# Moved weight splits and a reordered opening of attention in a gated cross-attention block

## The reference, cut to what matters

```python
x = x + tanh(g_xattn[0]) * xattn(layernorm(x), ctx, ctx, Wq, bq, Wk, bk, Wv, bv, interference, amp, Wo, bo)
x = x + tanh(g_ffn[0]) * ffn(layernorm(x), W_org, lora_down, lora_up, lora_keys, Wq)
...
def xattn(q, k, v, ...):
    qh, kh, vh = (interfere(proj(t, W, b)) for t, W, b in ...)   # x @ W.T + b, then a 4x4 mix per head
    weights = softmax(einsum('bhqdm,bhkdm->bhqkm', qh, kh) / sqrt(dk), axis=3)
    out = einsum('bhqkm,bhkdm->bhqdm', weights, vh)
    return out.reshape(b, s, dm) @ Wo.T + bo
```

## Time and profile before

| | us |
|---|---|
| median of the runs | 1349.94 (1349.28 to 1350.39) |
| profiled execution, its own time | 1349.01 |
| span of the profiled execution | 1347.2 |
| PE busy in the span | 1327.0 |
| DVE / POOL / ACT busy | 704.2 / 566.8 / 409.4 |

### The profile page before, as it was taken

How to read it: one execution, slowest core, us unless ns; L and a number is a source line. 1 busy time by engine, 2 the same in 40 slices (tenths; PEclk the granted TensorE clock), 3 DMA queues, 4 the chain that set the end, 5 groups by cost and what they waited for, 6 DMA issues and landing times.

```text
span 1347.2 us, 22259 instructions
## 1 busy us (share of the span) xinstructions
PE 1327.0 (98%) x8352; PEld 1117.8 (83%) x8352; DVE 704.2 (52%) x1371; ACT 409.4 (30%) x743; POOL 566.8 (42%) x777
## 2 busy tenths in 40 slices
PE   9999999999989999999999999999999999999999
PEld 8888878888778888788888888888788888888887
DVE  5423433455554545576777777777966144253110
ACT  3312221112112122355555565555551020111100
POOL 0899999999700000446666565565600000000000
PEclk9999999999989999999999999999999999999999
DMA  7897736345247666899897887777542202211011
GB/s 240 255 323 210 195 80 203 141 167 177 94 137 186 179 178 150 251 309 252 231 232 234 235 235 222 220 219 223 187 180 110 79 16 94 79 63 63 32 40 55
DMA packets 188939, 228.17 MB, mean 169 GB/s; under 512 B 26528, under 2 KB 124960, under 8 KB 188832
## 3 DMA queue, kind: packets, MB, share of 16 engines
q1 hardware_dynamic: 162096, 188.07, 46.7%
q10 hardware_dynamic: 26736, 38.68, 9.7%
HBM read 141.74 MB, written 83.89 MB: 167 GB/s over the span
## 4 chain that ended last, share of the span: by engine, by line
PE 70%; POOL 23%; DVE 2%; issue 2%; DMA 1%; ACT 1%; SPq 0%; ACTq 0%; POOLq 0%; DVEq 0%
PE bank L160 13%; PE bank L162 13%; PE bank L161 13%; POOL mixed_part L786 10%; POOL mixed_sum L793 6%; PE bank L1463 5%; PE bank L1483 4%; PE bank L1498 4%; PE bank L1444 4%; PE bank L1445 4%; PE bank L1446 4%; POOL mixed_sum L786 4%; PE bank L350 2%; POOL value_in L793 2%; PE bank L1470 1%
## 5 line engine op out<-in xcount | busy, mean ns | idle before, releaser
L1649 DVE TRANSPOSE_TENSOR_REDUCE part<-bank 128x16 f32<-128x512 f32 x256 | 174.3, 692 | 4.3 <-PE bank L1463 1.9
L1595 ACT ACTIVATE probT<-bank 128x512 f32<-128x512 f32 x256 | 138.9, 595 | 91.0 <-PE bank L1483 87.4
L1444 PE MATMUL bank<-w_hi,oT_hi 128*128 128x512 f32 x256 | 109.2, 426 | 3.0 <-POOL oT_lo L1769 2.9
L1265 DVE SCALAR_TENSOR_TENSOR raw_d<-bank,gates,raw_d 128x512 f32<-128x512 f32 x32 | 24.0, 750 | 162.9 <-PE bank L162 162.9
L576 DVE SCALAR_TENSOR_TENSOR stage_lo<-bank,bias_mixed,stage_hi 128x512 fp32r<-128x512 f32 x46 | 34.4, 750 | 128.7 <-ACT stage_hi L578 128.7
L160 PE MATMUL bank<-place_b,place_a 128*128 128x512 f32 x256 | 100.8, 394 | 0.9 <-DVE place_c L153 0.9
L160 PE MATMUL bank<-place_a,w_hi 128*128 128x512 f32 x256 | 100.4, 392 | 1.0 <-DVE place_a L153 1.0
L1445 PE MATMUL bank<-w_lo,oT_hi 128*128 128x512 f32 x256 | 101.2, 395 | 0.0
L1446 PE MATMUL bank<-w_hi,oT_lo 128*128 128x512 f32 x256 | 101.1, 395 | 0.0
L160 PE MATMUL bank<-w_hi,yT_hi 128*128 128x512 f32 x256 | 100.9, 394 | 0.0
L161 PE MATMUL bank<-place_c,place_a 128*128 128x512 f32 x256 | 100.1, 391 | 0.0
(11 more groups left out here) (241 smaller groups left out, 3088.3 us busy)
## 6 DMA issues: line engine op xcount, KB each, us to landing
k_rows<-stage_hi SPq DMA_DIRECT2D x128, 128.0 KB, 2.7
v_pad<-v_out SPq DMA_DIRECT2D x32, 512.0 KB, 2.8
v_place<-v_pad ACTq DMA_DIRECT2D x64, 256.0 KB, 4.2
tin<-in_ctx_cols SPq DMA_DIRECT2D x26, 512.0 KB, 4.2
k_in<-k_rows SPq DMA_DIRECT2D x64, 192.0 KB, 3.0
q_in<-q_rows SPq DMA_DIRECT2D x128, 96.0 KB, 3.3
q_rows<-wq_own SPq DMA_DIRECT2D x81, 128.0 KB, 2.5
raw_d<-x_mid SPq DMA_DIRECT2D x17, 512.0 KB, 3.3
```

The lines of the kernel that those rows point to most:

```text
L1444: pe.matmul(o_bank[out][:], hi[:, c, :], wo_hi[:, k, cols], start=(k == 0), stop=False)
L1595: act.activation(probT[o % NPT][:, i].rearrange("k a p q -> k (a p q)"), two_bank[i][:], ACT.Exp).then_inc(s_exp, 1)
L1649: dve.tensor_reduce(part[o % NS][:, :, 2 * i:2 * i + 2, :].rearrange("k a p b -> k a (p b)"), one_bank[i][:].rearrange("k (a b t) -> k a b ...
```

## The change

Five edits. The splits of the query weights stand at value products 4, 5, 7, 9, 10, 12, 14, 15 (before: 6 to 13). `wo_chunk` of the last query group stands ahead of the next query product (before: behind it). In slots 0 to 2 all three late steps stand ahead of the next first pass and the fold (before: two, with the third behind the fold). `WO_SLOTS` are 1, 5, 8, 11, 15, 18 (before: 1, 4, 7, 10, 14, 17), with SP's loads moved along. On POOL the subtraction for Wo stands behind `o_norm` and `oT_lo` of the slot (before: ahead of them). The load of `bo_row` stays in its slot, 7.

```diff
--- before.py
+++ after.py
@@ -812,12 +812,13 @@
                         value_chunk(2 * c + 1)
                 k_end[g] = len(line.jobs)
             keys_end = len(line.jobs)
+            QUERY_AT = (4, 5, 7, 9, 10, 12, 14, 15)
             for j, b in enumerate(VALUE_ORDER):
                 v_job(b, 0)
                 if j >= NB - GB:
                     x_norm(j - NB + GB, line.jobs[-1])
-                if 6 <= j < 6 + KC:
-                    query_chunk(j - 6)
+                if j in QUERY_AT:
+                    query_chunk(QUERY_AT.index(j))
                 v_job(b, 1)
                 if j < NB - GB:
                     ctx_jobs(NB + j)
@@ -836,6 +837,8 @@
             products_of = []
             for g in range(NG):
                 for c in range(KC if g + 1 < NG else KC - LATE):
+                    if g == NG - 1 and c:
+                        wo_chunk(c - 1, products_of[c - 1])
                     job = q_job(g, c)
                     if g + 1 < NG:
 
@@ -845,8 +848,6 @@
                             x_jobs((g + 1) * GB + (1, 3, 5, 6).index(c))
                     else:
                         products_of.append(len(line.jobs))
-                        if c:
-                            wo_chunk(c - 1, products_of[c - 1])
                     if (g, c) == (NG - 1, 0):
 
                         def zero_queries(dve):
@@ -993,7 +994,7 @@
 
             FREE_SLOTS = (0, 1, 2, 3, 4, 5, 6, 8, 9, 10, 12, 13, 14, 15)
             late_end = [FREE_SLOTS[(8 * j + 7) // 3] for j in range(LATE)]
-            WO_SLOTS = [1] + [e + 2 for e in late_end]
+            WO_SLOTS = [1] + [e + 3 for e in late_end]
             WO_TILES = (0, 1, 0, 0, 0, 0)
 
             def late_at(s):
@@ -1412,7 +1413,7 @@
                                 sp.wait_ge(s_wolo, 2 * (1, 3, 4, 5)[i - 2])
                             n = KC - LATE - 1 + i
                             sp.dma_start(wo_raw[WO_TILES[i]][:], wo_rows[n * P:(n + 1) * P, :]).then_inc(s_wo[WO_TILES[i]], 16)
-                    if s == WO_SLOTS[1] + 3:
+                    if s == WO_SLOTS[1] + 2:
                         sp.wait_ge(s_wolo, 2 * 2)
                         sp.dma_start(bo_row[:], bo.partition_broadcast(P)).then_inc(s_bo, 16)
                     late_store(sp, s, 0)
@@ -1525,7 +1526,7 @@
                         fold(s)
                     for part_of in work[:(len(work) + 1) // 2]:
                         project(*part_of)
-                    for step in late[:2]:
+                    for step in late[:2 + (s < LAG)]:
                         late_step(*step)
                     second_pass(s - LAG)
                     if h is None:
@@ -1533,7 +1534,7 @@
                         fold(s)
                     for part_of in work[(len(work) + 1) // 2:]:
                         project(*part_of)
-                    for step in late[2:]:
+                    for step in late[2 + (s < LAG):]:
                         late_step(*step)
                     if s in EARLY_JOBS:
                         line.run_tensor(pe, *EARLY_JOBS[s])
@@ -1749,13 +1750,6 @@
                         pool.tensor_tensor(neg[at][32:64], negmax[at][:], neg[at][0:32].bitcast(F32),
                                            ALU.subtract).then_inc(s_nlo, 1)
                         pool.wait_ge(s_nlo, s + 1)
-                    for half in range(2):
-                        if s - half in WO_SLOTS:
-                            i = WO_SLOTS.index(s - half)
-                            n, cols = KC - LATE - 1 + i, slice(half * HALF, (half + 1) * HALF)
-                            pool.wait_ge(s_wohi, i + 1)
-                            pool.tensor_tensor(wo_lo[:, n, cols], wo_raw[WO_TILES[i]][:, cols],
-                                               wo_hi[:, n, cols].bitcast(F32), ALU.subtract).then_inc(s_wolo, 1)
                     h = half_at(s, 5)
                     if h is not None:
                         pool.wait_ge(s_inv, h + 1)
@@ -1769,6 +1763,13 @@
                         pool.tensor_tensor(oT_lo[h % 2][:].rearrange("p a b -> p (a b)"), o_norm[:],
                                            oT_hi[h % 2][:].rearrange("p a b -> p (a b)").bitcast(F32),
                                            ALU.subtract).then_inc(s_olo, 1)
+                    for half in range(2):
+                        if s - half in WO_SLOTS:
+                            i = WO_SLOTS.index(s - half)
+                            n, cols = KC - LATE - 1 + i, slice(half * HALF, (half + 1) * HALF)
+                            pool.wait_ge(s_wohi, i + 1)
+                            pool.tensor_tensor(wo_lo[:, n, cols], wo_raw[WO_TILES[i]][:, cols],
+                                               wo_hi[:, n, cols].bitcast(F32), ALU.subtract).then_inc(s_wolo, 1)
                     for out, lag in ((0, O_LAG + 3), (1, O_LAG + 5)):
                         h = half_at(s, lag)
                         if h is not None and h % 2:
```

## The result

The changed kernel takes 1343.45 us in the median of 9 runs (1340.49 to 1346.87); the kernel before, beside it, 1349.91 (1346.83 to 1357.38). The ratio is 0.9949, with a 95% interval of 0.9934 to 0.9963: 5.0 to 8.9 us faster, where 12.4 had been forecast. The profiled execution took 1340.49 us, with a span of 1338.7. It is the fastest of the nine, so its trace shows less of the shortfall than the median has.

What follows compares the result with a forecast made beforehand. PE was taken to bound the kernel, busy 1327.0 of 1347.2 us, losing time at three waits. Terms 8.6 + 0 + 3.8 = 12.4 us off 1349.01 gave 1336.6, or 1337.5 as median; range 1334 to 1342.5.

Steps and rivals of the forecast that it cites:

- Query splits: Value products: PE's wait for the layer norm at product 14 and the slow clock behind it go, 8.6 us gained.
- `wo_chunk` and the three late steps: Slots 0 to 3: the 1.97 us wait goes, waits of 1.4 and three of 0.65 come; +0.6 us net.
- Wo splits one slot later: Slots 5, 8, 11, 15, 18: slot 8 costs 0 to 1.9, taken as 0.6, so slots 0 to 10 come out even.
- the last one: Last Wo load, behind SP's standstill in slot 16: lands near the short end, 3.7 us, and causes no wait.
- the opening was forecast to gain 3.8: Attention's opening: slots 0 to 10 even, then 5.3 recovered less a new wait of 1.5, 3.8 us gained.
- The 5.3 of slot 14: Slots 15 to 18: 5.3 us lost to PE's wait for `oT_lo` and slow clock, recovered by POOL's new order.
- The wait that I set against it, 1.5: Start of slot 17: new PE wait of 1.5 us for DVE's L1690, behind ACT and DVE work of slots 15 and 16.
- the clock falls behind a new wait: Rival: new waits at slots 0 or 16 lower the clock; 1339 to 1340.5 us, both up to 1342.5; chance 0.25.
- one of 2 us costs about as much again: PE's clock: a wait of about 1 us costs itself, one of 2 us about as much again in slow clock.
- the last Wo load is late: Rival: landing of 6.3 instead of 3.7 makes slot 20's second pass wait 1.5 to 2; 1339 to 1341 us; chance 0.11.
- the largest term: The query splits' gain in the value products, 8.6 us, two thirds of the sum.
- the new waits of slots 0 to 3 and 17: PE waits 1.4 for DVE's L576 in slot 0, 0.5 to 0.7 for L1690 in slots 0 to 2, about 1.5 at slot 17.

Runs made afterwards that it cites:

- e2: Changed kernel with the query splits back at products 6 to 13, so only attention's opening is changed; ratio 0.9998 against the kernel before.
- e3: Changed kernel with Wo splits back in slots 4, 7, 10, 14, 17 and the bo_row load's slot kept at 7; ratio 0.9908.
- e8: Changed kernel, every Wo split's halves together, last two splits back in slots 14, 17, third late step first in slot 0 alone, bo_row product in slot 11; no ratio given.
- e10: Changed kernel loading half the key rows for octets 9 to 24, output not the reference's; opening 92.75 us where the changed kernel took 93.08.
- e13: Second run of e2, the kernel with only attention's opening changed; ratio 1.0016 against the kernel before.
- e6: Changed kernel with DVE's product of bo_row in slot 11 instead of 9; whole time not told from the changed kernel's.
- e4: Changed kernel with both halves of the fifth Wo split on POOL in slot 15; ratio 0.9913 against the kernel before.
- e11: e4 loading half the key rows for octets 9 to 24, output not the reference's; opening 89.56 us, as e4.
- e12: Changed kernel with the last Wo load issued by ACT in slot 17 instead of by SP in slot 16; ratio 0.9919.
- e15: Changed kernel with the edits of e4 and e12 together; as good as e4 in time, opening 92.82 us.
- e16: e15 with the third late step first in slot 0 alone and the bo_row product in slot 11; ratio 0.9898, the fastest.
- e9: The kernel before, run once more unchanged for a second trace; opening 91.72 us where its first trace took 92.74.
- e14: Second run of e1, the kernel with the query splits alone; ratio 0.9919 against the kernel before.
- e1: The kernel before with only the query splits moved to products 4, 5, 7, 9, 10, 12, 14, 15; ratio 0.9930.
- e7: e1 plus POOL's Wo split behind oT_lo, nothing else; time not told from that of the query splits alone.

## Why the prediction was right or wrong

**Query splits: right.** 8.6 forecast, 45.94 - 37.34 = 8.60 measured, the same to 0.02 in each of fourteen traces; wait and slow clock went together.

**`wo_chunk` and the three late steps: right in mechanism.** The forecast waits were 1.4 and three of 0.65; they are 1.09 and three of 0.37 in every trace with this edit as it stands. Slots 0 to 6 gained the 0.6 in after (25.09 - 24.45 = 0.64). In seven traces (e2, e3, e8, e10 to e13) it went again, and in four of them 0.5 to 1.4 more, to a wait of 0.36 to 1.76 for a store of `neg` in slot 4. In those seven the store reached PE 6.5 to 7.7 us after its issue; in after PE took it 5.9 us after its issue without a wait.

**Wo splits one slot later: the size was off.** I took 0.6 for slots 8 to 10 out of a bound of 0 to 1.9. It was 0 in 6 of 9 traces and 1.7 to 2.9 in 3, more than the bound allowed, and not by the load that I looked at (Wo's) but by that of `bo_row`.

**The step that failed is the last one: "The queue is empty when it goes on, as before, so I take the landing near the short end, 3.7, and no wait."** I had named SP's standstill and what queues behind it, and then priced the Wo load alone. That load did no harm. The stores behind it did, the small ones of `neg` and the last one of late queries: SP's issues take 2.7 us of a slot of 3.1, so of the 3.7 us by which it is late for octet 16 it has made up only a third by slot 20, where it issues the store for octet 19 2.4 us after it could. Means over the traces show it as a transfer: slots 15 to 18 fall from 16.73 (four traces with the old order on POOL) to 14.18 (the fourteen others), 2.55 gained; slots 19 to 22 rise from 12.27 (the same four) to 14.95 (after twice, e2, e13, e6, e10), 2.7 lost. Where the stop is shortened or avoided (e4, e11, e12, e15, e16), they are at 12.86; e8, with stops of 0.7 and yet 14.75, is the exception told above. In after the opening was forecast to gain 3.8 and lost 0.34, 4.1 short: 2.7 of that are in slots 19 to 22, 1.1 in slots 7 to 10 and 0.3 in slots 15 to 18.

**The 5.3 of slot 14 was one execution's.** I made the sum against one trace and took its loss there for the program's. Slots 15 to 18 took 18.09, 15.51, 15.53 and 17.78 in the four traces with the old order, so the loss was 2.7 to 5.3 by the working of that step. The wait that I set against it, 1.5, was 1.63.

**The rivals.** That the clock falls behind a new wait did not happen in after: 1.00 behind 1.63 and 2.47. So the working "one of 2 us costs about as much again" does not hold for every wait (the last section has more). That the last Wo load is late: ACT waited 1.50 for it, with no wait of PE for the exponentials in slot 20. What came was a rival that I had not formed. The direction, the largest term and the new waits of slots 0 to 3 and 17 were right.

## What to carry to other kernels

When an engine that only issues transfers has to wait for another engine, price everything that is queued behind the wait, the smallest stores too, and see whether that engine has slack in a slot to catch up. A moved step that removes a wait on one engine can set a longer one on another, here six slots later. And before a loss is counted as gain, see it in a second trace: the value part as changed, where PE waits for no landing, repeats to 0.02 us; the opening, where it does, differed between two traces of one program by 0.0, 1.0, 3.3 and 4.9.

## What the runs showed of the hardware that was not expected

**The same wait, two clocks.** PE's wait in slot 0 was 1.97 in before, e9 and e14 and 1.96 in e1 and e7. Stretches behind it, of e7 and of e1 (the granted clock is the number ahead of the DMA share):

```profile
547.00:549.00 2.00, 2.00 (x8) 1.71 (x8) 0.90 (x2) 0.00 (x0) 1.88 (x3) 0.50 0.67 71
```

```profile
544.00:546.00 2.00, 2.00 (x13) 1.73 (x11) 1.23 (x2) 0.00 (x0) 1.70 (x4) 1.00 0.90 145
```

So the length of a wait alone did not decide: 1.96 (e7), 1.97 and 3.23 (e13) were followed by 0.50, the 1.2 GHz level, and 1.96 (e1) and 2.47 by 1.00, the 2.4 GHz level. The Trainium skill (TensorE: Matmul & The Clock Gate, section "HAM oscillation — how this bites in real kernels") puts this to the length of the gap against a bound; here gaps below it fall on both sides. Slots 0 to 6 took 24.97 in e7 and 25.05 in e1, so the low clock cost nothing in the sum there: e1, whose PE was not slowed, waited another 0.60 and 0.32 in slot 4.

**The first 17 us.** PE's first products took twice as long in some executions, while the granted clock's row read 1.00: the same 16 matmuls of e6 and of after,

```profile
9.55 3.41 PE L646 MATMUL bank<-bcol,mix 128*128 128x2 f32 x16
```

```profile
7.86 1.84 PE L646 MATMUL bank<-bcol,mix 128*128 128x2 f32 x16
```

and the value part then began at 347.49 and 342.64. That is 4.9 us between two executions whose code is the same up to there, as much as most differences between the changed kernels of the table.

**DVE beside POOL.** The product of `bo_row` on DVE took 1.68 in after, where it began behind a `w_lo` of POOL (1.29 from 572.23 on), and 0.73 to 0.77 in the seventeen other traces. In e13 it began ahead of `w_lo`, and `w_lo` took 1.68:

```profile
583.31 0.75 DVE L1696 TENSOR_SCALAR bo_row<-bo_row,gates 128x1024 f32<-128x1024 f32 x1 [0.45 <-DMA bo_row<-in_bo]
```

```profile
583.53 1.68 POOL L1771 TENSOR_TENSOR w_lo<-wo_raw,w_hi 128x512 fp32r<-128x512 f32 x1
```

The Trainium skill (SBUF — State Buffer, section "SBUF: two separate sides") calls the port that the two share "an exclusive lock, not a bandwidth split"; the trace agrees as far as spans on POOL can tell: whichever began second took longer, in after DVE's, which ended 0.55 behind POOL's, and in e13 POOL's, which ended 1.15 behind DVE's.
